# Four attention layers on one core: the second layer's MLPs behind its attention in three products, its attention on two slots of four PSUM banks

## What is computed

```python
# L0: attention over channels, then + x
# L1: latents = x, keys and values from concat([ctx, x]) : 256 keys, 16 heads of 16
attn = softmax(where(mask, einsum('bkhd,bnhd->bhkn', q, k) / 16, -inf))
y = einsum('bhkn,bnhd->bkhd', attn, v) @ out_w + out_b + x
x = gelu(rmsnorm(y) * w @ mlp_w1 + mlp_b1) @ mlp_w2 + mlp_b2 + x     # 256 -> 1024 -> 256
# L2: two cross attentions of 16 heads of 128 (with a bias key), then an MLP 256 -> 1024 -> 256
# L3: self attention, cross attention, MLP
```

## Time and profile before

| | |
|---|---|
| median of 3 runs | 2255.97 us (2251.94 to 2257.0) |
| the profiled execution | 2245.47 us |
| its span, first to last instruction | 2242.7 us |
| PE busy | 2010.5 us, 90% |
| DVE, ACT, POOL busy | 1037.4, 983.4, 687.4 us |
| mean granted clock of PE | 0.954 of full |
| on the chain that ended last | PE 77%, DVE 9%, ACT 8% |

### The profile page before, as it was taken

The page is one execution under the profiler, slowest core; times in us unless marked ns, Lnnn a source line. Parts: engine busy times, 40 slices in busy tenths (PEclk is TensorE's granted clock), DMA queues, the critical chain, the costliest instruction groups (busy, mean ns, idle before and its releaser), DMA issues.

```text
span 2242.7 us, 38803 instructions
## 1 busy us (share of the span) xinstructions
PE 2010.5 (90%) x15917; PEld 1654.0 (74%) x15917; DVE 1037.4 (46%) x1889; ACT 983.4 (44%) x2563; POOL 687.4 (31%) x803
## 2 busy tenths in 40 slices
PE   7878797987899999999999999999969978887798
PEld 4556565655788888888888888888857756666587
DVE  3443323214444444445444444444355377767743
ACT  3323344362344444443333444444424366666643
POOL 2311202014232232413323232231112066757600
PEclk9977898998999999999999999999979989999999
DMA  4000000001000000000001000000020010000000
GB/s 130 20 2 6 6 1 1 1 1 52 19 20 20 10 29 1 21 10 20 1 20 38 10 20 20 11 1 1 1 86 1 8 41 2 6 1 6 2 10 29
DMA packets 28178, 38.40 MB, mean 17 GB/s; under 512 B 1745, under 2 KB 19809, under 8 KB 28001
## 3 DMA queue, kind: packets, MB, share of 16 engines
q1 hardware_dynamic: 28000, 35.93, 5.0%
HBM read 33.83 MB, written 2.10 MB: 16 GB/s over the span
## 4 chain that ended last, share of the span: by engine, by line
PE 77%; DVE 9%; ACT 8%; issue 2%; POOL 2%; DMA 1%; SPq 0%; DVEq 0%; ACTq 0%; POOLq 0%
PE ps L192 40%; PE ps_four L2444 5%; PE ps_four L2464 5%; PE ps_four L192 3%; PE ps_four L2453 3%; ACT l_pt L1600 2%; PE ps L2260 2%; PE ps_four L2190 2%; PE ps L2340 2%; PE ps L2298 1%; PE ps L2249 1%; PE ps_four L2211 1%; PE ps L2228 1%; PE ps L2236 1%; DVE l_mt L1782 1%
## 5 line engine op out<-in xcount | busy, mean ns | idle before, releaser
L1703 ACT ACTIVATE l_prob<-ps_four,l_mx 128x129 f32<-128x129 f32 x512 | 181.4, 367 | 576.0 <-DVE l_mx L2031 576.0
L1499 POOL TENSOR_TENSOR l_prob<-l_prob,l_mx 128x516 f32<-128x516 f32 x128 | 134.1, 1048 | 748.5 <-DVE l_mx L2038 748.5
L192 PEld LDWEIGHTS ps<-l_wo,l_ao 128*128 128x128 f32 x1536 | 199.7, 191 | 17.6 <-DVE l_ao L2050 6.8
L192 PE MATMUL ps<-ctxT,l_wk 128*128 128x512 f32 x768 | 211.0, 410 | 0.0
L192 PE MATMUL ps<-l_wo,l_ao 128*128 128x256 f32 x1536 | 206.0, 284 | 5.5 <-DVE l_ao L2050 5.5
L192 PE MATMUL ps<-l_hT,l_wq 128*128 128x512 f32 x768 | 209.9, 409 | 0.0
L192 PE MATMUL ps<-l_wv,ctxT 128*128 128x512 f32 x768 | 202.7, 399 | 1.7 <-ACT l_qT L1684 1.4
L1465 POOL TENSOR_TENSOR l_sm<-l_sm,l_mask 128x1024 f32<-128x1024 f32 x64 | 150.2, 2370 | 119.0 <-DVE l_sm L1996 118.9
L192 PEld LDWEIGHTS ps<-l_wv,ctxT 128*128 128x128 f32 x768 | 141.9, 188 | 45.1 <-ACT l_qT L1684 10.2
L192 PEld LDWEIGHTS ps<-ctxT,l_wk 128*128 128x128 f32 x768 | 136.0, 190 | 23.1
L192 PEld LDWEIGHTS ps<-l_hT,l_wq 128*128 128x128 f32 x768 | 135.2, 189 | 22.7
(11 more groups left out here) (266 smaller groups left out, 3921.5 us busy)
## 6 DMA issues: line engine op xcount, KB each, us to landing
l_staging<-in_L_xattn_wv SPq DMA_DIRECT2D x8, 512.0 KB, 3.7
l_staging<-in_L_xattn_wk SPq DMA_DIRECT2D x8, 512.0 KB, 3.7
l_staging<-in_L_xattn_wq SPq DMA_DIRECT2D x8, 512.0 KB, 4.2
l_staging<-in_L_xattn_wo SPq DMA_DIRECT2D x8, 512.0 KB, 3.8
x_tok<-in_x SPq DMA_DIRECT2D x4, 512.0 KB, 7.6
ctx_tok<-in_ctx SPq DMA_DIRECT2D x4, 512.0 KB, 6.0
l_mlp_w<-in_L_xattn_mlp_w SPq DMA_DIRECT2D x2, 1024.0 KB, 8.8
l_w<-in_L_xattn_w_fc SPq DMA_DIRECT2D x2, 1024.0 KB, 6.6
```

What stands on the lines that cost most here:

```text
L192: ins = e.matmul(out, a, b, start=start and i == 0, stop=stop and i == 2, skip_group_check=not check)
L1499: e.tensor_tensor(pr[:, :, 0:S + 1], pr[:, :, 0:S + 1], mx[:, 3, :].unsqueeze(2).to_broadcast([P, GB, S + 1]), ALU.mult).then_inc(sem("poo ...
L1703: ins = e.activation(pr.t[:, b, 0:S + 1], banks[b // 2].t[:, (b % 2) * (S + 2):(b % 2) * (S + 2) + S + 1], ACT.Exp, bias=mx[:, 1, b:b + 1] ...
```

## The change

1. **PSUM.** Banks 4 to 7 become a second slot of four, `ps_high`. `maxima(n, 0)` stays in `ps_four`; `maxima(n, 1)` and both `probs` go to `ps_high`. All single-bank products of the attention, `over_v` and the transposes among them, go to banks 0 to 3, in turn. So `maxima(n, 0)` waits until those four banks are empty, and each single-bank product behind it waits for DVE: banks 0 and 1 for the first half of its maximum (which DVE now takes in two instructions), banks 2 and 3 for the second.
2. **Order.** Per item it is now: maxima(n, 0), probs(n-1, 1), fill, fill, maxima(n, 1), over(n-1), fill, shift, heads(n+1), fill, probs(n, 0), fill. The second half of an item's probabilities comes an item earlier than `over` did, so the loop is one round shorter.
3. **MLPs.** `mlp32` is gone. All four MLPs run behind the attention through `mlp_split`, on banks 0, 1, 4, 5, beside the last group's end (banks 2, 3, 6, 7), the loading of L2's weights, three of L2's norms and its first values. The MLP weights are loaded late in the attention (into memory that L1's inputs held) and split on DVE.
4. **Rates.** `L1_RATE` (0.9, 2.6, 2.6, 2.2) becomes (0.7, 1.0, 1.0, 0.9), since the MLPs' stages are gone from `rest`.

```diff
-L1_RATE = (0.9, 2.6, 2.6, 2.2)
+L1_RATE, L1_SLACK = (0.7, 1.0, 1.0, 0.9), 1
+L2_SLACK = 2
...
+        self.ps_high = self.ctx.enter_context(nc.psum_tensor("ps_high", [P, 4, 512], F32))
+        self.high_slot = Slot(self.ps_high, pl.sem("pe.high_full"), pl.sem("any.high_empty"))
...
-        four, over = Ring([self.four_slot]), self.banks(4)
-        self.tr = self.misc = self.side = self.banks(5, 6, 7)
+        four, high = Ring([self.four_slot]), Ring([self.high_slot])
+        low = self.bank_slots[0:4]
+        over = self.tr = self.misc = self.side = self.banks(0, 1, 2, 3)
...
-            pl.bank(four, "four", n, "max", j)
-            pl.emit("l1_max", n, j)
+            pl.bank((four, high)[j], "four", n, "max", j)
+            pl.emit("l1_max", n, j, emptied=[(slot.empty, slot.uses) for slot in low] if j == 0 else ())
             pl.free("four", n, "max", j)
+            if j == 0:
+                for i, slot in enumerate(low):
+                    slot.after = (pl.sem("dve.l1_max:a"), n + 1) if i < 2 else (self.four_slot.empty, self.four_slot.uses)
...
-            pl.bank(four, "four", n, "prob", s)
+            pl.bank(high, "four", n, "prob", s)
...
-            yield from self.mlp32(t, ("hs", t), h_done, self.plain["mlp_w1"], self.plain["mlp_w2"], b1, ACT.Gelu_apprx_tanh,
-                                       ("sp.l1_plain", 48))
+        def mlp(g):
+            t = ("l1", g)
+            yield from self.mlp_split(t, "l1", b1, ACT.Gelu_apprx_tanh, (lambda: mlp_in(g + 1)) if g + 1 < G else None)
             self.x_done[g] = self.x_add(t, g, t, ("pool.x_bias", t))
...
+        self.l1_mlps = [self.within(mlp(g), self.banks(0, 1, 4, 5), self.work, self.st, "dve.norm_xn") for g in range(G)]
+        self.l1_last = self.within(chain(weights, last), self.banks(2, 3, 6, 7), self.work, self.st, "dve.norm_xn")
         while ("out32", ("l1", G - 1), 1) not in pl.place:
-            next(last)
+            next(self.l1_mlps[0])
+            next(self.l1_last)
         self.barrier("l2a")
...
-        run(until_norm(self.l1_last))
-        first = normalise(0, 0)
-        interleave(self.l1_last, chain((next(first) for _ in range(4)), alternate(first, load_weights(0, 0)), first_values(),
-                                       normalise(0, 1), normalise(0, 2)), 2.7)
+        interleave(self.l1_mlps[0], chain(self.l1_last, load_weights(0, 0)), 2.0)
+        interleave(self.l1_mlps[1], chain(normalise(0, 0), first_values()), 1.7)
+        interleave(self.l1_mlps[2], normalise(0, 1), 1.4)
+        interleave(self.l1_mlps[3], normalise(0, 2), 1.4)
...
+            e.tensor_reduce(out[:, 0:2], scores[:, 0:2], AX.X, ALU.max, negate=True).then_inc(sem("dve.l1_max:a"), 1)
+            e.tensor_reduce(out[:, 2:4], scores[:, 2:4], AX.X, ALU.max, negate=True).then_inc(bk.slot.empty, 1)
```

More of the change, by code:

```diff
@@ L47, in __init__ @@
     def __init__(self, t, full=None, empty=None):
-        self.t, self.full, self.empty = t, full, empty
+        self.t, self.full, self.empty, self.after = t, full, empty, None
         self.taken, self.uses, self.fills, self.freed = False, 0, 0, None
@@ L55, in __init__ @@
     def __init__(self, slot):
-        self.slot, self.t, self.n, self.before = slot, slot.t, slot.uses, slot.freed
+        self.slot, self.t, self.n, self.before, self.after = slot, slot.t, slot.uses, slot.freed, slot.after
 class Ring:
@@ L501, in plan_l1 @@
         pl.free("l1_out_bias")
[L502 removed]
+        begun, ready, h_done = {}, {}, {}
         def begin(g):
@@ L544, in values @@
             ready[g] = ("empty", "rows", ("l1_v", g, 1), 1)
+            if g == G - 1:
+                pl.emit("l1_mlp_loads", after=("full", "rows", ("l1_v", g, 1), 1))
         def heads(n):
@@ L636, in fill @@
                 next(rest, None)
-        last = end(G - 1)
+        last, weights = end(G - 1), self.mlp_weights("l1", ("sp.l1_mlp", 32), (("w1", 0), ("w1", 1), ("w2", 0), ("w2", 1)))
         heads(0)
-        for n in range(B + 2):
-            if n >= B:
-                next(last)
+        for n in range(B + 1):
             if n < B:
                 maxima(n, 0)
-            if n >= 2:
-                while (n - 2) // GB not in ready:
-                    next(rest)
-                over_v(n - 2, 0)
+            else:
+                next(last)
+            if n > 0:
+                probs(n - 1, 1)
+            fill(n)
             fill(n)
@@ L651, in plan_l1 @@
                 maxima(n, 1)
-            if n >= 2:
-                over_v(n - 2, 1)
+            else:
+                next(weights)
+                next(weights)
+            if n > 0:
+                while (n - 1) // GB not in ready:
+                    next(rest)
+                over_v(n - 1, 0)
+                over_v(n - 1, 1)
             fill(n)
-            if 1 <= n <= B:
-                probs(n - 1, 0)
             if n < B:
                 run(shifted(n))
-            fill(n)
-            if 1 <= n <= B:
-                probs(n - 1, 1)
             if n + 1 < B:
@@ L745, in mlp_split @@
                 yield
+            if k == FC and beside is not None:
+                yield from beside()
     def plan_l2_attention(self, scope):
@@ L904, in output @@
                 weights_ahead.append(load_weights(*nxt))
-        def until_norm(stages):
-            while ("norm_tr", ("l1", G - 1), DC - 1) not in pl.place:
-                yield next(stages, None)
         def first_values():
@@ L2099, in fill @@
             q.wait_ge(u.slot.empty, u.n)
+            if u.after is not None:
+                q.wait_ge(*u.after)
             return u
@@ L2196, in l1_shift @@
             mt = use["mt", n].t
-            q.wait_ge(*pl.event(("empty", "four", n, "max", 1)))
+            for j in range(2):
+                q.wait_ge(*pl.event(("empty", "four", n, "max", j)))
             bk = fill("shift", n)
@@ L2291, in norm_tr @@
             ins.then_inc(bk.slot.full, 1)
-        def mlp_down(m, k):
-            f, hid = self.mlps[m], use["hid32", m, k].t
-            q.wait_ge(*pl.event(("empty", "up32", m, k)))
-            banks = [fill("side", m, i) for i in range(2)]
-            for b in range(GB):
-                ins = e.matmul(banks[b // 2].t[:, (b % 2) * D:(b % 2 + 1) * D], hid[:, b * S:(b + 1) * S], f["w2"][:, k, :],
-                               start=k == 0 and b % 2 == 0, stop=k == FC - 1, skip_group_check=True)
-            ins.then_inc(sem("pe.mlp_down"), 1)
         def cols(p, j):
```

160 lines of the change are left out of this document (75 added, 85 removed).

## The result

The changed kernel takes 2201.85 us, the median of 4 runs (2199.37 to 2207.65), beside 2256.41 us for the kernel before on the same chip. The ratio is 0.9766, with a 95% interval of 0.9742 to 0.9791. The profiled execution took 2199.37 us.

What follows compares the result with a forecast made beforehand. No engine is full in the attention; PE waits and runs at its lower clock. Attention 288 plus 112 us behind it make 400 against 456.1, 56 less: 2256 - 56 = 2200 us, range 2165 to 2236.

Steps and rivals of the forecast that it cites:

- the text's own sum: Whole kernel: the profiled execution of 2245.5 us less 56 us gives 2189.5 us.
- Part 1, the attention: L1's attention: 266 us at 2.4 GHz plus clock losses, 288 us against 401.3 before.
- The walk's waits: Attention, items priced step by step: PE waits 2.28 us for ACT, 1.3 for DVE's second half-maximum, 1.6 for DVE's copies.
- The low clock of sparse items: Attention: six sparse items lose about 3 us each to the low clock, less in two, 17 us in all.
- the 22 us charged in all: Attention, low clock: 17 us for six sparse items and 5 us for ten dense ones.
- Part 2, behind it: Last `over` to L2's first query product: PE work 100.7 us plus stalls, 112 us, 57 more than before.
- The weights' split: Behind the attention: MLP weights split on DVE, 8.2 us in all, of which PE stalls 3 us.
- the stall per MLP: Behind the attention: a norm or addition on DVE ahead of a step's bank stalls PE 2 us an MLP, 8 in all.
- that sign: Behind the attention: MLPs take 24 to 26 us each; the forecast is wrong if one is over 28.
- The first, the low clock: Attention at 1.2 GHz, some 450 us, result 2362; slower from 344 us on; chance 6%, half way another 10%.
- The second rival: Clock stays up, no stalls behind the attention: 369 us for both stretches, 87 us less, 2169; chance 20%.
- The third, worse waits: New waits worse than walked: 1 us on 32 MLP steps or 2 us on 16 items, 2232; chance 10%.

Runs made afterwards that it cites:

- experiment 7: Changed kernel with POOL's heads of the next item written ahead of this item's output: 2201.51 us, ratio 0.9778 to the kernel before.
- the repeat: The changed kernel run again without an edit, on the chip of three other runs: 2195.31 us, ratio 0.9778 to the kernel before.
- experiment 11: Changed kernel with an item's first maximum taken in one reduction of four banks instead of two: 2205.64 us, ratio 0.9816 to the kernel before.
- experiment 3: Changed kernel with one slot of four and the old order of attention stages, MLPs behind in three products: 2210.64 us, ratio 0.9835 to the kernel before.
- experiment 2: Changed kernel with one slot of four banks again, new order and MLPs behind the attention kept: 2269.07 us, ratio 1.0092 to the kernel before.
- experiment 6: Kernel before with its MLPs' Gelu left out (ACT copies with the bias, no function table loaded): 2238.43 us, ratio 0.995 to the kernel before.

## Why the prediction was right, and where it was not

**The total.** Forecast 2200, measured 2201.85. The forecast was 56 us less; the ratios 0.9766 and 0.9778 say 50 to 53. Between the profiled executions the difference is 46.1 us, between the medians 54.6: the profile of before lay 10.9 us below its median, that of after 2.5 below. So a part of the closeness is that a slightly large gain met a slightly high median, and that is luck. Against the profiled execution the text's own sum was 2189.5 us, and 2199.4 came. The last `over` ended at 395.1 us and L2's first query product started at 516.3, where the text had 398 and 510.

**Part 1, the attention.** Forecast 288 us, measured 285.7 and 293.0, at mean clocks of 0.92 and 0.90 (forecast 0.87 to 0.95). The walk's waits are there: ACT in front of the second maxima 2.2 us each, DVE's second half-maximum in front of projections 1.6 us each, the readers `l_kT` and `l_vv` in front of the first maxima. One was missed: POOL's heads queue behind the item's output, 12.0 us in 7 waits. The step that failed is the list of new waits, which had none on POOL. It did not decide, since experiment 7 shows that most of it covers a wait for ACT. The low clock of sparse items, charged at 3 us each, measured 3.3 in the item shown, but not in every sparse item: the products by the values took 1.95 or 1.96 us in eleven of the sixteen items and 3.3 to 3.6 in five; in the repeat 1.95 or 1.96 in nine and 3.2 to 3.6 in seven, not all of them the same. So the 22 us charged in all came out near enough as a sum (285.7 and 293.0 less 266 are 19.7 and 27.0, POOL's waits included), and not item by item. The text's 'busy 8.6 of 13.4 us' is 8.8 by its own prices, which changes nothing. Splitting the first maximum, which the text only used for its 1.3 us wait, is worth some 0.4% (experiment 11).

**Part 2, behind it.** Forecast 112 us, measured 121.2. PE's work there was put at 100.7 and is 105.5. Of this, some 3 us are two first steps at the low clock, 12 products in 4.57 and 4.58 us, where a step's 6 products otherwise take 1.55. Idle time was put at 11 and is 15.7 us. The weights' split, put at 3, cost 2.7 (1.9 and 0.8). The term that was too small is the stall per MLP, 2 us of DVE work ahead of a step's bank and 8 in all: the waits are 8.5 and 4.4 us, and the low clock behind them is on top. What happened in the larger part is another wait. The first step of an MLP needs the bank of the sums before it, and DVE adds those to x only behind the split of the next input. PE waits 4.05, 1.71 and 2.77 us for that, and behind the first and the third wait it runs at the low clock. From first step to first step the MLPs took 36.1, 29.9, 28.2 and 26.9 us (the first with the output projection and the barrier behind it inside, the last up to L2's first query product). The text had 24 to 26, and called itself wrong above 28; by that sign it was wrong. The sentence forgot the output projection, norms and values that its own sum puts beside the MLPs: its 112 us are 28 an MLP. The first seam is the longest for a reason of its own, DVE and POOL in order of time:

```profile
425.48 1.52 POOL L1440 TENSOR_TENSOR l_wq<-l_staging,l_wq 128x512 fp32r<-128x512 f32 x1
...
425.89 1.67 DVE L1973 TENSOR_TENSOR l_mhs<-l_hs,l_mhs 128x512 fp32r<-128x512 f32 x1
...
428.11 1.31 POOL L1440 TENSOR_TENSOR l_wq<-l_staging,l_wq 128x512 fp32r<-128x512 f32 x1
428.35 1.62 DVE L1973 TENSOR_TENSOR l_mhs<-l_hs,l_mhs 128x512 fp32r<-128x512 f32 x1
...
431.31 4.57 PE L195 MATMUL ps_four<-l_mhs,l_w 128*128 128x512 f32 x12 [4.05 <-DVE x_tok L1950]
...
458.14 0.69 DVE L1973 TENSOR_TENSOR l_mhs<-l_hs,l_mhs 128x512 fp32r<-128x512 f32 x1
```

The subtraction takes 0.69 us, and 1.67 and 1.62 where POOL is splitting L2's weights. The text put the split of L2's weights at nothing, with MLP 0 as its cover; that was not quite so.

**What the gain is made of.** "The loss is PE waiting, and PE at the lower of its two clocks": the walk of the items put 1.2 us an item (14.6 to 13.4) on the first. In the attention PE's idle time fell from 65.0 us to 58.9, and it rose by 4.4 behind it. The steps differ: with the MLPs moved and on one slot it was 55.5 to 55.8, so the new order on two slots waits a little more than the old one on one, and what it gains it gains by the clock. By parts the runs divide the gain so, undone in this order: the move of the MLPs (with the lower rates and the smaller edits named in experiment 3) 0.86%, three products 0.79% (0.96 to 1.08% when they are undone first), two slots with their order 0.57 to 0.69%. The order alone, on one slot, would have lost 2.6%.

**The rivals.** The first, the low clock, did not come: 0.92 where it needed about 0.7. It can come, though: the kernel of experiment 2 has 357.8 us of attention at 0.78 and is 0.92% slower than before, beyond the 344 us at which the text put the turning point. There it is not the clock alone, as the rival has it: PE is also idle 34 to 35 us more than in the changed kernel, and the mean clock did not fall to 0.7. The rule cited with it, from the Trainium skill (TensorE: Matmul & The Clock Gate, "A second HAM failure mode: psum-queue depth-cycling"), is borne out in kind by that run; in the changed kernel PE idles more of the attention than before (21% against 16%) and yet has the higher clock. The second rival needed no stalls behind the attention and the high clock within it, and neither came. The third, worse waits, came by 9 us in part 2 only, its low clock included.

**What stays open.** The part behind the first query product is 4.8 us longer, just inside the 5 us of the forecast. It was 1677.6 to 1685.0 us in the other kernels with the MLPs behind the attention, 1681.3 again in the repeat, and 1678.2 in experiment 6, where it is the code of before. For the same 11414 products PE is busy 5.8 us more and idle 1.0 us less, and it comes late: 1433.8 us behind the first query product, 9405 of them are done where before it was 9420, and from there to the end the mean clock is 0.95 where it was 0.97. No run isolated the cause.

## What to carry to other kernels

Work that fills the gaps of a loop can cost more there than its own time, so ask for that price before leaving it in: here three MLPs cost some 17 us extra, about half of it by 27 table loads, since two functions took turns on ACT. A new order can need the buffers that came with it: on one slot it lost 2.6% against the old order. (The slots with the old order were not tried.) And a wait that stands in the profile can be free: taking 6.8 us from POOL's moved them to ACT, one step later. Last, repeat a profile before you explain a difference of a few us by it.

## What was unexpected of the hardware

- **The same program, another clock.** Two profiled executions of the changed kernel with nearly equal waits differ by 7.3 us in the attention: over 239 to 311 us the granted clock was 0.98 in one and 0.89 in the other.
- **DVE and POOL on SBUF.** A subtraction of 128x512 with both inputs in SBUF took 0.69 us alone, and 1.67 and 1.62 us where POOL's subtraction had begun 0.41 and 0.24 us earlier. DVE's ended 0.56 and 0.55 us after POOL's, as if it had started only then. The Trainium skill (SBUF — State Buffer, "SBUF: two separate sides") says that a DVE instruction with two SBUF inputs and a GpSimd instruction that reads SBUF share a port pair, which the one that starts first holds for its whole instruction while the other is blocked. The trace agrees, in the two pairs shown.
